# Paired input transposes, a new ScalarE order in the down-weight jobs, and filter tables without GpSimd

## The reference

```
K = 2 * Re( sum_n Ct[h,n] * exp(dtA[h,n] * l) )            # l = 0..1023, per channel h
y = causal_convolution(x, K) + x * D                        # by FFT in the reference
y = y * (l < length[b])
xq = fake_quant(y);  gate = xq @ fake_quant(w_gate).T ; up = xq @ fake_quant(w_up).T
out = x + fake_quant(silu(gate) * up) @ fake_quant(w_down).T   # w_gate, w_up: [2752, 1024]; w_down: [1024, 2752]
```

## Time and profile before

| | before |
|---|---|
| median of 3 runs | 1339.59 us (1338.51 to 1340.16) |
| profiled execution, its own time | 1339.14 us |
| span of its trace | 1336.9 us |
| PE busy | 1263.6 us (95%) |
| PEld busy | 686.5 us (51%) |
| DVE busy | 918.1 us (69%) |
| ACT busy | 409.0 us (31%) |
| POOL busy | 345.0 us (26%) |
| filters, to the first `turn_x` | 0 to 59.5 us |
| convolution and weights | 59.5 to about 422 us |
| feed-forward | 427.4 to 1336.9 us |

### The profile page before, as it was taken

How to read it: one execution, slowest core, us unless ns; L and a number is a source line. 1 busy time by engine, 2 the same in 40 slices (tenths; PEclk the granted TensorE clock), 3 DMA queues, 4 the chain that set the end, 5 groups by cost and what they waited for, 6 DMA issues and landing times.

```text
span 1336.9 us, 20250 instructions
## 1 busy us (share of the span) xinstructions
PE 1263.6 (95%) x6837; PEld 686.5 (51%) x6932; DVE 918.1 (69%) x1536; ACT 409.0 (31%) x593; POOL 345.0 (26%) x326
## 2 busy tenths in 40 slices
PE   2499999999996999999999999999999999999997
PEld 0377777776664444444444444444444444444443
DVE  7677877777884865677656777566776567765675
ACT  2244444444451222322222222222222222222322
POOL 3333333324450122221122211222112131122220
PEclk9799999999998999999999999999999999999999
DMA  3279999997974132323323333223332223322323
GB/s 98 75 243 265 273 265 266 271 296 240 264 221 158 32 68 67 71 67 87 74 62 71 71 77 84 61 69 73 78 84 61 69 69 74 86 67 65 71 60 79
DMA packets 137595, 161.52 MB, mean 121 GB/s; under 512 B 101645, under 2 KB 101855, under 8 KB 136287
## 3 DMA queue, kind: packets, MB, share of 16 engines
q1 hardware_dynamic: 137566, 161.16, 44.7%
HBM read 113.28 MB, written 25.49 MB: 104 GB/s over the span
## 4 chain that ended last, share of the span: by engine, by line
PE 67%; issue 0%; DVE 0%; ACT 0%
PE ps_g L1062 23%; PE ps_u L1062 22%; PE ps_o L1088 22%; PE ps_o L1095 1%; PE ps_t L1072 0%; ACT h_t L1197 0%; DVE ps_o L1149 0%; DVE res L1152 0%
## 5 line engine op out<-in xcount | busy, mean ns | idle before, releaser
L1226 POOL TENSOR_TENSOR h_int<-h,rounder 128x512 bf16<-128x512 f32 x186 | 174.4, 952 | 706.2 <-ACT h L1188 703.4
L1062 PE MATMUL ps_g<-wgu,rows 128*128 128x512 bf16 (+1 forms) x1516 | 327.1, 358 | 5.9 <-PEq L413 4.9
L1062 PE MATMUL ps_u<-wgu,rows 128*128 128x512 bf16 (+1 forms) x1493 | 324.4, 356 | 2.3
L1088 PE MATMUL ps_o<-wd,h_t 128*128 128x512 bf16 x1314 | 294.0, 379 | 1.8 <-issue 0.2
L1182 ACT ACTIVATE g_buf<-g_buf 128x512 f32<-128x512 f32 x192 | 112.3, 585 | 583.7 <-DVE g_buf L1120 583.7
L1120 DVE SCALAR_TENSOR_TENSOR g_buf<-ps_g,sx_all,wide 128x512 f32<-128x512 f32 x192 | 132.3, 689 | 229.6 <-PE ps_g L1062 229.6
L853 PE MATMUL ps_y<-u,toep 128*128 128x512 f32 (+7 forms) x1024 | 268.6, 416 | 2.4 <-ACT s_rows L722 1.0
L1062 PEld LDWEIGHTS ps_g<-wgu,rows 128*128 128x128 bf16 x1536 | 145.2, 98 | 163.5 <-issue 13.2
L1062 PEld LDWEIGHTS ps_u<-wgu,rows 128*128 128x128 bf16 x1536 | 147.0, 98 | 151.6 <-issue 1.0
L853 PEld LDWEIGHTS ps_y<-u,toep 128*128 128x128 f32 x1024 | 176.9, 191 | 89.3 <-issue 57.9
L1088 PEld LDWEIGHTS ps_o<-wd,h_t 128*128 128x128 bf16 x1346 | 131.1, 98 | 151.9 <-issue 1.1
(11 more groups left out here) (141 smaller groups left out, 657.6 us busy)
## 6 DMA issues: line engine op xcount, KB each, us to landing
toep<-k_rev SPq DMA_DIRECT2D x64, 512.0 KB, 5.7
res<-in_x SPq DMA_DIRECT2D x64, 256.0 KB, 3.9
out_x<-res SPq DMA_DIRECT2D x64, 256.0 KB, 3.2
wide<-in_L_ffn_w_gate SPq DMA_DIRECT2D x22, 512.0 KB, 6.6
wide<-in_L_ffn_w_up SPq DMA_DIRECT2D x22, 512.0 KB, 8.4
wide<-in_L_ffn_w_down SPq DMA_DIRECT2D x8, 1376.0 KB, 8.5
rows<-in_x SPq DMA_DIRECT2D x32, 256.0 KB, 6.6
x_more<-in_x SPq DMA_DIRECT2D x32, 256.0 KB, 7.0
```

What stands on the lines that cost most here:

```text
L1062: last = pe.matmul(bank[:, 0:n], xq[:, par, c, :], wgu[:, NC - 1 - c, first + cols.start:first + cols.stop], start=(c == 0), stop=(c == NC ...
L1088: last = pe.matmul(ps_o[o][:], h_t[0:width, c, :], wd[0:width, c, o * W:(o + 1) * W], start=(c == 0), stop=(c == FC - 1))
L1226: pool.tensor_tensor(h_int[:, piece(j)], h[:, par, piece(j)], rounder[:].to_broadcast([P, n]), ALU.subtract).then_inc(h_int_ready, 1)
```

## The change

1. **Input transposes in pairs.** `turn_x` no longer turns each channel's 64 rows alone, 8 transposes of 64 x 128 for each. It turns all 128 rows at once, 4 transposes of 128 x 128 for each of two halves of the length, so 8 for a tile instead of 16. Both halves are turned after convolve 0, ahead of `turn_w` and of `turn_max`; after convolve 1 comes `turn_w` and then `spread_inv`. `u` gets a second buffer. `take_u` sorts the channels apart while it copies, both copies come early in the ScalarE body, and `convolve` waits for both of its tile.
2. **ScalarE order in down jobs.** The places 0 and 1 of unit i now come ahead of `round_down(i+1)`.
3. **Filter tables.** VectorE makes `decay` and `high_im` itself, GpSimd does nothing there any more; the squares of the cosine table move to ScalarE (`Square`); factors are folded (8.0 for 2.0 in the weights, 0.5 steps in the tables).

```diff
-                tick(dve.scalar_tensor_tensor(out=s(part), in0=s(part), scalar=2.0, in1=s(NORM), op0=ALU.mult, op1=ALU.mult))
+                tick(dve.scalar_tensor_tensor(out=s(part), in0=s(part), scalar=8.0, in1=s(NORM), op0=ALU.mult, op1=ALU.mult))
...
+            for kind in range(2):
+                tick(dve.tensor_tensor(decay[:, kind], over(0), powers[:, kind], ALU.mult))
+            reached["decay"] = count[0]
...
-                dve.wait_ge(act_sines, 2 * half + 2)
+                dve.wait_ge(act_sines, 3 * half + 3)
...
-                tick(dve.scalar_tensor_tensor(out=co, in0=co, scalar=-2.0, in1=co, op0=ALU.mult, op1=ALU.mult))
-                tick(dve.scalar_tensor_tensor(out=co, in0=co, scalar=1.0, in1=de, op0=ALU.add, op1=ALU.mult))
-
-                tick(dve.tensor_tensor(si[:, 0], si[:, 0], de[:, 0], ALU.mult))
-                reached["powers", half] = count[0]
-                tick(dve.scalar_tensor_tensor(out=si[:, 1], in0=si[:, 1], scalar=-1.0, in1=de[:, 1],
-                                              op0=ALU.mult, op1=ALU.mult))
+                tick(dve.scalar_tensor_tensor(out=co, in0=co, scalar=0.5, in1=de, op0=ALU.subtract, op1=ALU.mult))
+                for kind, sign in ((0, -0.5), (1, 0.5)):
+                    tick(dve.scalar_tensor_tensor(out=si[:, kind], in0=si[:, kind], scalar=sign, in1=de[:, kind],
+                                                  op0=ALU.mult, op1=ALU.mult))
...
+                tick(dve.tensor_tensor(t0, co[:, 0], over(3)[:, hs], ALU.mult))
+                tick(dve.tensor_tensor(t1, si[:, 0], over(2)[:, hs], ALU.mult))
+                tick(dve.tensor_tensor(high_im[:, hs], t1, t0, ALU.add))
...
-            pool.wait_ge(dve_step, reached["cols"])
-            for kind in range(2):
-                pool.tensor_tensor(decay[:, kind], over(0), powers[:, kind], ALU.mult).then_inc(pool_step, 1)
-            for half, hs in enumerate(halves):
-                pool.wait_ge(dve_step, reached["powers", half])
-                pool.tensor_tensor(phase[:, 0, hs], cosine[:, 0, hs], over(3)[:, hs], ALU.mult).then_inc(pool_step, 1)
-                pool.tensor_tensor(phase[:, 1, hs], sine[:, 0, hs], over(2)[:, hs], ALU.mult).then_inc(pool_step, 1)
-                pool.wait_ge(pool_step, 3 * half + 4)
-                pool.tensor_tensor(high_im[:, hs], phase[:, 1, hs], phase[:, 0, hs], ALU.add).then_inc(pool_step, 1)
...
+                act.wait_ge(act_sines, 3 * half + 2)
+                act.activation(cosine[:, :, hs], cosine[:, :, hs], ACT.Square).then_inc(act_sines, 1)
...
-        u = sb("u", [P, 2, NC * B])
+        u = sb("u", [P, 2, 2, NC, B])
...
-            def take_u(i, hh):
-                act.wait_ge(x_turned, 2 * i + hh + 1)
-                if not isinstance(i, int) or i >= 1:
-                    act.wait_ge(conv_done, 2 * i + hh - 1)
-                act.activation(u[:, hh, :], ps_x[hh][:], ACT.Copy).then_inc(u_done, 1)
+            def take_u(i, par, k):
+                half = slice(k * NC // 2, (k + 1) * NC // 2)
+                act.wait_ge(x_turned, 2 * i + k + 1)
+                if not isinstance(i, int) or i >= 2:
+                    act.wait_ge(conv_done, 2 * i - 2)
+                act.activation(u[:, par, :, half, :], ps_x[k][:].rearrange("p (c h b) -> p h c b", h=2, b=B),
+                               ACT.Copy).then_inc(u_done, 1)
...
                 if has(i, TILES - 1):
-                    take_u(i + 1, 0)
-                if not gate_stage(i) and has(i, WEIGHT_ITERS - 1):
-                    round_down(i + 1, 1 - par)
+                    take_u(i + 1, 1 - par, 0)
+                    take_u(i + 1, 1 - par, 1)
...
                     place_w(i, par, 0)
                     place_w(i, par, 1)
+                if not gate_stage(i) and has(i, WEIGHT_ITERS - 1):
+                    round_down(i + 1, 1 - par)
...
-            def turn_x(i, par, hh):
-
-                rows = slice(hh * B, (hh + 1) * B)
-                for c in range(NC):
-                    last = pe.transpose(ps_x[hh][:, c * B:(c + 1) * B], x_bufs[par][rows, c * P:(c + 1) * P], ident[rows, rows])
+            def turn_x(par, k):
+                for c in range(NC // 2):
+                    first = (k * NC // 2 + c) * P
+                    last = pe.transpose(ps_x[k][:, c * P:(c + 1) * P], x_bufs[par][:, first:first + P], ident[:])
                 last.then_inc(x_turned, 1)
...
-                pe.wait_ge(u_done, 2 * i + hh + 1)
+                pe.wait_ge(u_done, 2 * i + 2)
...
-                    if not last_one:
+                    if not last_one and hh == 0:
                         await_x(i + 1, 1 - par)
+                        for k in range(2):
+                            turn_x(1 - par, k)
+                    if gate_stage(i) or down_stage(i):
+                        turn_w(i, par, hh if gate_stage(i) else 2 * hh)
+                        if hh == 0 and not gate_stage(i):
+                            turn_w(i, par, 1)
                     if not isinstance(i, int) or i >= 1:
                         if hh == 0:
                             turn_max(i - 1)
                         else:
                             spread_inv(i - 1)
-                    if not last_one:
-                        turn_x(i + 1, 1 - par, hh)
-                    if gate_stage(i) or down_stage(i):
-                        turn_w(i, par, hh if gate_stage(i) else 2 * hh)
-                        if hh == 0 and not gate_stage(i):
-                            turn_w(i, par, 1)
```

More of the change, by code:

```diff
@@ L139, in long_filters @@
         act_small = sem("act_small")
-        pool_step = sem("pool_step")
         pool_products = sem("pool_products")
@@ L276, in _ @@
             tick(dve.tensor_copy(cols[:], ps_cols[:]))
-            reached["cols"] = count[0]
+            for kind in range(2):
+                tick(dve.tensor_tensor(decay[:, kind], over(0), powers[:, kind], ALU.mult))
+            reached["decay"] = count[0]
             for half, hs in enumerate(halves):
@@ L286, in _ @@
                 dve.wait_ge(act_decay, 1)
-                dve.wait_ge(act_sines, 2 * half + 2)
+                dve.wait_ge(act_sines, 3 * half + 3)
                 co, si, de = cosine[:, :, hs], sine[:, :, hs], decay[:, :, hs]
-                tick(dve.scalar_tensor_tensor(out=co, in0=co, scalar=-2.0, in1=co, op0=ALU.mult, op1=ALU.mult))
-                tick(dve.scalar_tensor_tensor(out=co, in0=co, scalar=1.0, in1=de, op0=ALU.add, op1=ALU.mult))
-                tick(dve.tensor_tensor(si[:, 0], si[:, 0], de[:, 0], ALU.mult))
-                reached["powers", half] = count[0]
-                tick(dve.scalar_tensor_tensor(out=si[:, 1], in0=si[:, 1], scalar=-1.0, in1=de[:, 1],
-                                              op0=ALU.mult, op1=ALU.mult))
+                tick(dve.scalar_tensor_tensor(out=co, in0=co, scalar=0.5, in1=de, op0=ALU.subtract, op1=ALU.mult))
+                for kind, sign in ((0, -0.5), (1, 0.5)):
+                    tick(dve.scalar_tensor_tensor(out=si[:, kind], in0=si[:, kind], scalar=sign, in1=de[:, kind],
+                                                  op0=ALU.mult, op1=ALU.mult))
                 t0, t1 = turns[:, 0, hs], turns[:, 1, hs]
-                tick(dve.tensor_tensor(t0, sine[:, 0, hs], over(3)[:, hs], ALU.mult))
-                tick(dve.tensor_tensor(t1, cosine[:, 0, hs], over(2)[:, hs], ALU.mult))
+                tick(dve.tensor_tensor(t0, si[:, 0], over(3)[:, hs], ALU.mult))
+                tick(dve.tensor_tensor(t1, co[:, 0], over(2)[:, hs], ALU.mult))
                 tick(dve.tensor_tensor(high_re[:, hs], t1, t0, ALU.subtract))
+                tick(dve.tensor_tensor(t0, co[:, 0], over(3)[:, hs], ALU.mult))
+                tick(dve.tensor_tensor(t1, si[:, 0], over(2)[:, hs], ALU.mult))
+                tick(dve.tensor_tensor(high_im[:, hs], t1, t0, ALU.add))
                 reached["tables", half] = count[0]
@@ L354, in _ @@
             flat = "p k h r -> p (k h r)"
-            act.wait_ge(pool_step, 2)
+            act.wait_ge(dve_step, reached["decay"])
             act.activation(decay[:].rearrange(flat), decay[:].rearrange(flat), ACT.Exp).then_inc(act_decay, 1)
@@ L384, in _ @@
                 pe.wait_ge(dve_step, reached["tables", half])
-                pe.wait_ge(pool_step, 3 * half + 5)
                 pe.wait_ge(d_added, 2 * half + 2)
@@ L687, in place_w @@
                 act.activation(wd[:, NC * k:NC * k + whole, cols], bank[:, 0:whole, :], ACT.Copy).then_inc(w_placed, 1)
-            for hh in range(2):
-                take_u(0, hh)
+            for k in range(2):
+                take_u(0, 0, k)
             round_gu(0, 0, 0)
@@ L710, in body @@
                     place_w(i, par, 1)
+                if not gate_stage(i) and has(i, WEIGHT_ITERS - 1):
+                    round_down(i + 1, 1 - par)
                 if gate_stage(i):
                     place_w(i, par, 0)
-                if has(i, TILES - 1):
```

(8 more changed lines are left out.)

## The result

The changed kernel takes 1315.93 us (median of four runs, 1313.27 to 1317.78) against 1339.73 us before (median of four, 1338.51 to 1340.16). The ratio is 0.9822, with a 95% interval of 0.9804 to 0.9841: 23.8 us faster where 20.8 were forecast. The span of its profiled execution is 1313.0 us, 23.9 less than 1336.9.

The account below looks back on a forecast made before the run. TensorE's own work was taken to bound the gate jobs, DMA just behind, and a cross-engine loop the down jobs. Savings 3.85 - 0.8 + 10.9 + 0.8 + 6.0 = 20.75 us gave 1318.8 us, range 1310 to 1328.

Parts of the forecast that it names:

- The wide transpose: `turn_x`: each 128-column transpose in a series costs 0.115 us, bounds 0.062 and 0.21; saves 0.54 us a tile.
- (c): Rival: the wide transpose costs 0.062 us and DMA stops the tile at about 10.2; 1315 us at most; chance 0.10.
- (d): Rival: a wide transpose costs 0.21 us or more in a series, kernel slower at 1343.3 us; chance 0.04.
- The gate body: Gate jobs: a tile body of 10.22 us against 10.77; 11.9 us saved over 22 bodies.
- VectorE's slack: Gate jobs: VectorE's idle ahead of the second mask falls from 1.81 to about 1 us a tile.
- DMA: Gate jobs: share reaches 1.00, saturated, but loads issued two tiles ahead carry the backlog; 1.0 us charged, bounds 0 to 8.
- rival (a): Gate jobs: DMA ceiling keeps the body at about 10.55 us; gate saves 4, not 10.9; 1325.5 us; chance 0.17.
- The down jobs: Down jobs: bodies fall from 12.21 to 11.2 us, about 6 us saved, bounds 0 and 11.
- the x load: Down jobs: its 1.8 us margin shrinks by 1.6 and the later round; body taken as 11.2 us.
- The loop through `xq` and GpSimd: Down jobs: `xq` rounding waits for GpSimd's second piece; coming ahead of it shortens the 12.21 us loop by 1.7.
- the ScalarE order: Down jobs: places ahead of `round_down`; nothing in the old loop, up to 1 us delay in a 10.6 us loop.
- The filters: Kernel start: tables done at 46.7 instead of 50.6 us, steps behind unchanged; 3.85 us saved, bounds 2.7 to 4.2.

Follow-up runs that it names:

- e11: The changed kernel itself run again, five runs: 1315.83 us; its profiled execution took 1319.37 us.
- e6: Changed kernel with SP's x load of tile i+2 issued at the start of its body, ahead of the wait for unrounded weights: 1313.78 us.
- e8: Kernel before with GpSimd's first two pieces of each w_down unit cut into instructions of 512 columns: 1334.03 against 1338.76 us.
- e3: Changed kernel with the old ScalarE order in the down jobs, `round_down` back ahead of places 0 and 1: 1324.62 us.
- e1: Kernel before with the new filter tables alone: 1336.82 against 1339.46 us.
- e5: Changed kernel with tile 1's Toeplitz loads issued behind the last store of the filters: 1316.84 us.
- e4: Changed kernel with `turn_max` and `spread_inv` back ahead of `turn_x` and `turn_w`, paired transposes kept: 1350.94 us.
- e9: Changed kernel with x load at the start of SP's body and tile 1's Toeplitz loads behind the last filter store: 1310.85 us.

## Why the prediction held, and where it did not

**The wide transpose** was the term on which most hung. 0.115 us was said, 0.110 measured, far from both bounds (0.062 and 0.21). The way to it held: the difference in length between 64 and 128 columns is the difference in spacing, and the length of a lone one is not its price in a series. Rivals (c) and (d) fall. The Trainium skill, "TensorE: Matmul & The Clock Gate", Part 4 (PE-mode transpose), gives some 275 ns for a 128 x 128 bf16 transpose inside a kernel. As the price of one in a series that figure does not hold here: for these f32 ones 273 ns is the length and 110 the cost.

**The gate body** was put at 10.22 and is 10.05. Of the 0.17, 0.12 is the convolve at 3.94 us. It has 4.00 where bf16 `turn_w` stands ahead of it (rows 2, and the second body of the changed kernel, where no `ps_m` or `ps_i` stands between) and 3.94 behind an f32 `ps_m` or `ps_i`. That the new order gives each convolve an f32 neighbour was not seen, so this part of the gain came by luck. Another 0.04 is the transposes (8 x 0.005). 22 x 0.72 = 15.8 less 13.2 leaves about 2.6 of losses, with 0.9 of them in the slow first body, which gained nothing, where 1.0 was charged in all. Most of the rest is in three bodies of 10.52, 10.81 and 10.55. The first body differs from one execution to the next (12.79 in this trace, 11.63 in e11's), so its 0.9 says little about the change.

**VectorE's slack** was put at about 1 us; the trace has 0.97 of idle ahead of `mask_y(i, 1)`, against 1.81 in rows 4.

```profile
134.00 0.69 DVE L768 TENSOR_TENSOR y<-ps_y,mask 128x512 f32<-128x512 f32 x1 [0.97 <-PE ps_y L846]
```

**DMA** was put at a share of 1.00 with the backlog carried, and so it is; rival (a) did not come, and TensorE waits for x once in the gate jobs, 0.55 us. But the text took 1.00 for saturated, and e6, with 0.93 at the same rate, shows that it was not.

**The down jobs** gave 9.1, not 6.0. The step that was off is the x load: 11.2 us a body was taken for all, and the margin does fail, but in two bodies out of eight (2.17 and 0.68 us), while most run at 10.39, TensorE's own work. The two waits cost 3.3 us in all. Other executions are less lucky: e11's profiled one has a down sum of 91.8, a saving of 4.7. So the forecast of 6.0 lies between two executions of the same kernel. In the sum for the x load, landings of 7.1 us would give (3.8 + 8.8 + 2 + 7.1) / 2 = 10.85 a body and not 10.6; nothing else rests on it. The loop through `xq` and GpSimd was read rightly (e8), and so was `xq` going in behind the first piece. What the text had wrong is the worth of the ScalarE order: it was costed as a delay of up to 1 us against no gain. e3 shows it as the condition of the whole gain, since `spread_inv` behind the third turn puts place 0 on the path.

**The filters** gave 2.1, not 3.85. The tables' own times hold to 0.2 us. The step that failed is that all behind the tables is a chain of unchanged steps: the last store does not cost the same as before, but queues behind four Toeplitz loads (2 MB) that are issued when half 0 is stored, and half 0 gained only 2.2. e1 and e5 show this. The Trainium skill, "ScalarE: Activation LUTs", section "Table sets: the hidden batching unit", does not name the square among the functions of every set. The sum with table loads around the squares gave 2.75, nearer to the 2.1, but by chance: the trace has no load there.

Two misses of opposite sign, 1.7 less in the filters and 4.9 more behind them, make up the 3 us between the forecast and the result. That the total came so near is in part their cancelling. Two small terms nearly cancel as well: the profiled execution's time is 3.23 above its span, not 2.24, and the median is 0.3 below that execution, not 0.45 above.

## What to carry to other kernels

Where a step stands in TensorE's own order can decide more than its price: with the same paired transposes the kernel is 24 us faster than before when the maximum's turn and the spread of the inverses stand behind the other turns, and 11 us slower than before with both in front (e4). Ask, for each short transpose or matmul that waits for a chain on another engine, what independent work can stand ahead of it, and move the engine that serves it (here ScalarE's places) at the same time. And follow a store up to the barrier through its DMA queue: what is issued ahead of it is part of its cost. Issue first the load that is needed first: with x early an earlier barrier showed in full (e6 to e9), and without it no gain could be seen (e5). A DMA share of 1.00 does not by itself say that the engines are full: a version that moves the same bytes in another order had 0.93. And take more than one trace before you book a gain of a few us to a stage, as the two traces of the changed kernel show.

## What the runs showed of the hardware that was not expected

An f32 convolve of 16 records takes 3.94 us behind an f32 transpose or matmul and 4.00 behind bf16 transposes. e4, which puts the bf16 turns back in front of the convolve, has 4.00 again (146.57 to 150.57). Why the 0.06 arises was not tried.

A VectorE rounding that comes while GpSimd runs waits for that instruction's end and then goes ahead of GpSimd's next, also where the next is already queued; GpSimd's pair is then longer by 0.45 us. Cutting GpSimd's instructions in two lowered the longest `xq` from 2.41 to 1.56 us (e8).

TensorE's granted clock stayed at 1.00 behind an idle of 2.17 us in the down jobs of one execution. Behind an idle of 2.80 in another it was 0.57 over the next 3.3 us, and the same eight transposes took 1.97 us, not 1.09.
